# Combining two expert results per token on TensorE in a two-layer attention and expert kernel

## The chip, the cores and the metric

The kernel runs on one core of a Trainium2 chip. The metric is device microseconds of one execution, as the median of three. Before the change that is 857.17 us (runs of 855.79 to 862.05).

## The reference, cut to what matters

Two layers follow each other on 2048 tokens of 192 channels (x is 8 x 16 x 16 x 192, fp32). Each layer is an attention with a residual, then a mixture of eight experts with a residual. Of every expert layer this is what bears on the change (the first layer's; the second also divides the two gates by their sum):

```python
gates = softmax(x_flat @ Wg + bg)
topk_g, topk_i = top_k(gates, 2)             # two experts per token
combine = zeros((n, 8)).at[arange(n)[:, None], topk_i].add(topk_g)
h = gelu(einsum('nd,edf->enf', x_flat, W1) + b1)
y = einsum('enf,efd->end', h, W2) + b2
out = einsum('ne,end->nd', combine, y)       # gate-weighted sum of two results
t = t + out                                  # residual
```

After the first expert layer the sum t is layer-normalised (mean and variance over 192 channels) and goes into the second attention. After the second one it is the output.

## The kernel before

One program holds all stages; each engine has one instruction stream in program order, and semaphores order the engines among themselves. Tokens lie on partitions: 16 tiles of 128 tokens, in 4 blocks of 4 tiles (512 tokens). `x_sb` holds the residual stream, 128 x 16 x 192, in SBUF for the whole run.

In an expert layer (`moe_*`, layer l = 0 or 1) tokens are sorted by expert into 39 tiles of 128 rows, worked on in 13 trips of 3 tiles by a loop (`grouped`, whose first and last trip are written out by hand). For each trip TensorE multiplies by W1 (L1446, L1454), ScalarE applies Gelu (`hidden_units`, L1498), TensorE multiplies by W2 (L1462), VectorE adds the bias (L1342), and GpSimd scatters the rows to `yd` in DRAM (L1534), two rows per token. When the last scatter has landed, SyncE issues four loads (L1202), one per block, that bring `yd` back as `yt` (128 x 16 x 2 x 192); each signals `y_in{b}`.

The combine is then VectorE's alone (L1379 to L1394): for each block, eight `scalar_tensor_tensor` of 128 x 192 compute x = y * gate + x, first the four tiles of the first expert, then the four of the second. In layer 0 VectorE also takes the block's moments at once (`ln_moments`, L258 to L266: statistics, their aggregation, variance plus epsilon), GpSimd raises that to -1/2 (L272), and while the next block is worked on VectorE finishes scale and offset of the block before (`block_scales`, L281 to L303). ScalarE normalises the block with these into `xn` (`block_normalise`, L312), TensorE transposes it (`ln_transpose`, L323, eight transposes), ScalarE copies the transpose to SBUF (`ln_copy`, L333), and TensorE computes q, k and v (L1827). Blocks alternate between two buffers and two pairs of PSUM banks. On TensorE's stream the four `ln_transpose` stand at the head of `attn1_tensor` (L1816 and L1817), where nothing else is between them. `ln_transpose(b)` waits for `xn_ready`, and from block 2 on for the copy of block b - 2; `block_normalise` of blocks 2 and 3 waits for the transposes of two blocks earlier.

In layer 1 nothing follows the combine but the stores: SyncE waits for `combined` of a block and issues its 384 KB to the output (L1987 to L1990).

Two patterns of the second attention are like those that the change uses: twelve matmuls by the identity over 512 columns that compute nothing needed (L1892, "filler" below), and the projection, whose result VectorE adds to `x_sb` from PSUM in one instruction per block (L1806), followed by the same moments and scales.

Of the kernel before, what the change touches and what calls it, by code (L numbers as in the profile page):

```python
# [21 lines left out]
F32 = mybir.dt.float32  # L22
F32R = mybir.dt.float32r
# [3 lines left out]
ALU = mybir.AluOpType  # L27
ACT = mybir.ActivationFunctionType
# [3 lines left out]
P = 128  # L32
IMGS, SIDE, C = 8, 16, 192
PIX = SIDE * SIDE
T = IMGS * PIX
TILES = T // P
KC = 96
BLKS = 4
BT = T // BLKS
TPB = BT // P  # L40
# [12 lines left out]
HC = 3  # L53
# [12 lines left out]
R_MAX = 114  # L66
# [7 lines left out]
E, F, FT = 8, 768, 768 // P  # L74
SLOTS = 42
MT = (2 * T - E) // P + E
# [7 lines left out]
def build(nc, a, out):  # L84

    ctx = ExitStack()
    with ctx:
        def sb(name, shape, dt=F32):
            return ctx.enter_context(nc.sbuf_tensor(name, shape, dt))
# [16 lines left out]
        x_sb = sb("x_sb", [P, TILES, C])  # L106
# [3 lines left out]
        cst = sb("cst", [P, a["cst"].shape[1]])  # L110
# [17 lines left out]
        qq = sb("qq", [P, 6144], F32R)  # L128
        kk = sb("kk", [P, 6144], F32R)
        pk = sb("pk", [P, NH, PADS], F32R)  # L130
        nm = sb("nm", [HC, 2, BT], F32R)

        gw = sb("gw", [P, 2, TILES])
        gidx = sb("gidx", [P, SLOTS], I32)
# [4 lines left out]
        rt = sb("rt", [P, 2816])  # L139
        totb = sb("totb", [P, 2, P], BF16)  # L140
        hotb = sb("hotb", [P, 2 * TILES * E], BF16)
        hotb_v = hotb[:, :].rearrange("p (c e) -> p c e", e=E)
        ROUTE_STEPS = [0]
        ps = ctx.enter_context(nc.psum_tensor("ps", [P, 8, 512], F32))

        at = 0
# [10 lines left out]
        def ar(word, shape, parts=P):  # L157

            n = 1
            for s in shape:  # L160
                n *= s
            v = arena[0:parts, word:word + n]
            names = "abcd"[:len(shape)]
            if len(shape) > 1:
                v = v.rearrange(f"p ({' '.join(names)}) -> p {' '.join(names)}",
                                **{k: s for k, s in zip(names, shape)})
            return v
# [50 lines left out]
        b2s = xn[:, :, :, :].rearrange("p u t c -> p (u t) c")  # L218

        yt = ar(0, [TILES, 2, C])  # L220

        q0 = qq[:, :].rearrange("p (c h n) -> p c h n", c=CPB, h=HC)
        k0 = kk[:, :].rearrange("p (c h n) -> p c h n", c=CPB, h=HC)
# [3 lines left out]
        def s_(name):  # L227
            if name not in S:
                S[name] = sem(name)
            return S[name]  # L230
# [85 lines left out]
        def ln_transpose(pe, b):  # L316

            pe.wait_ge(s_("xn_ready"), BLKS + b + 1)
            if b >= 2:
                pe.wait_ge(s_("tp_free"), b - 1)  # L320
            for k in range(2):
                for j in range(TPB):
                    last = nc.tensor.transpose(ps[0:KC, b % 2 * 2 + k, j * P:(j + 1) * P],  # L323
                                               xn[:, b % 2, j, k * KC:(k + 1) * KC], ident)
            last.then_inc(s_("xn_free"), 1)
# [175 lines left out]
        def attn0_sync(sp):  # L501
            def load(b, cc):

                G = b * CPB + cc
                if b:
                    sp.wait_ge(s_("st_done"), (G - CPB + 1) * HC * UNITS)
                else:
                    sp.wait_ge(s_("k_rows"), cc + 1)
                sp.wait_ge(s_(f"kept_a{b}"), 8 * 16)
                if cc >= 2:  # L510
                    sp.wait_ge(s_(f"kept_b{b}"), 8 * 16)
                hs = slice(cc * HC, (cc + 1) * HC)
                for r, lo, hi in ((0, 0, 32), (R_DUP, 0, HD), (R_REL2, 32, QLO), (R_LO, QLO, QDROWS)):
                    sp.dma_start(q0[r:r + hi - lo, cc].bitcast(F32), qd[b, lo:hi, hs]).then_inc(s_(f"chunk_in{cc}"), 16)
                for r, lo in ((R_HI, 0), (R_DUP, HD), (R_LO, 0)):
                    sp.dma_start(k0[r:r + HD, cc].bitcast(F32), kd[b, lo:lo + HD, hs]).then_inc(s_(f"chunk_in{cc}"), 16)

            def minus_max(G):
                cc = G % CPB
                sp.wait_ge(s_(EMPTIED["m", G][0]), EMPTIED["m", G][1])  # L520
                sp.dma_start(q0[R_MAX:R_MAX + 1, cc].bitcast(F32), nm[0:HC, G % 2, :].bitcast(F32))\
                    .then_inc(s_(f"nm_in{cc}"), 16)

            for kind in ("t0", "t2", "r0", "r1"):
                sp.wait_ge(s_("split"), split_at(kind, 0))
                store(sp, kind, 0)
            sp.wait_ge(s_("q_rows"), CPB + 1)
            for cc in range(CPB - 1):
                load(0, cc)
            minus_max(0)  # L530
            load(0, CPB - 1)
            for b in range(BLKS):
                ahead = b + 1 < BLKS
                minus_max(b * CPB + 1)
                if ahead:
                    load(b + 1, 0)
                minus_max(b * CPB + 2)
                if ahead:
                    load(b + 1, 1)
                minus_max(b * CPB + 3)  # L540
                if ahead:
                    load(b + 1, 2)
                    minus_max(b * CPB + 4)
                    load(b + 1, 3)
            first_matrices(sp, 0, 0, E)
# [60 lines left out]
        def attn0_vector(v):  # L606
# [11 lines left out]
            def minus(G):  # L618

                v.wait_ge(s_("misc_full"), FULL["m", G])  # L620
                nc.vector.tensor_scalar(nm[0:HC, G % 2, :], ps[0:HC, BANK["m", G], :], -1.0, None, ALU.mult)\
                    .then_inc(s_("dve_emptied"), 1)

            def values(b, g):
# [530 lines left out]
        def product(r):  # L1155

            return ps[:, 2 * r, 0:C]

        def arrived(r):

            return ps[:, 6 + r // 2, r % 2 * 2 * P:(r % 2 + 1) * 2 * P].rearrange("p (k n) -> p k n", k=2)

        def grouped(eng, body):

            body(0, True, False)
            with eng.Fori(1, TRIPS - 1) as trip:
                body(trip, False, False)
            body(TRIPS - 1, False, True)
# [37 lines left out]
        def moe_vector(v, l):  # L1206
# [117 lines left out]
            if l == 1:  # L1324
# [2 lines left out]
                step(vec.reciprocal(total, total))  # L1327
                step(vec.tensor_tensor(gw[:], gw[:], total.unsqueeze(1).broadcast_to([P, 2, TILES]), ALU.mult))
            ROUTE_STEPS[0] = count[0] if l == 0 else ROUTE_STEPS[0]

            n0 = l * MT
# [44 lines left out]
                clear_columns(v)  # L1377

            for b in range(BLKS):  # L1379
                v.wait_ge(s_(f"y_in{b}"), 16 * (l + 1))  # L1380
                for k in range(2):
                    if k:
                        v.wait_ge(s_("first_added"), l * BLKS + b + 1)
                    for t in range(b * TPB, (b + 1) * TPB):
                        last = vec.scalar_tensor_tensor(x_sb[:, t], yt[:, t, k], gw[:, k, t:t + 1], x_sb[:, t],  # L1385
                                                        ALU.mult, ALU.add)
                    last.then_inc(s_("combined" if k else "first_added"), 1)
                if l == 0:
                    v.wait_ge(s_("combined"), b + 1)
                    ln_moments(v, 2, range(b, b + 1))  # L1390
                    if b:
                        block_scales(v, 2, b - 1)
# [3 lines left out]
        def moe_tensor(pe, l):  # L1396
# [68 lines left out]
            def body(trip, first, last):  # L1465
# [8 lines left out]
                for r in range(3):  # L1474
                    down(n + r, r)

            pe.wait_ge(s_("w_in"), 16 * 25 * (l + 1))
            pe.wait_ge(s_("te_ready"), l + 1)
            for r in range(3):
                gathered(n0 + r, 0, r)  # L1480
            grouped(pe, body)

        def moe_scalar(act, l):
            if l == 0:
                nx_copy(act, l, BLKS - 1)
            act.wait_ge(s_("shifted"), l + 1)
            nc.scalar.activation(rt[:, 4 * TILES * E:5 * TILES * E], rt[:, 2 * TILES * E:3 * TILES * E], ACT.Exp)\
                .then_inc(s_("exp_gates"), 1)
            if l == 0:
                clear_edges(act)  # L1490
            nc.scalar.activation(credit[0:1, 8:9], credit[0:1, 0:1], ACT.Gelu)

            def hidden_units(n, r):
                e = act.value_load(te[0:1, bass.ds(n - l * MT, 1)], min_val=0, max_val=E - 1)
                act.wait_ge(s_("up_done"), n + 1)
                act.wait_ge(s_("down_done"), n)
                for f in range(FT):
                    last = nc.scalar.activation(hidT[r][:, f, :], hidden(r, f), ACT.Gelu,  # L1498
                                                bias=b1s[l][:, bass.ds(e * FT + f, 1)])
                last.then_inc(s_("hid_ready"), 1)  # L1500

            def body(trip, first, last):
                for r in range(3):
                    hidden_units(l * MT + trip * 3 + r, r)

            act.wait_ge(s_("te_ready"), l + 1)
            grouped(act, body)
            if l == 0:
                nc.scalar.activation(credit[0:1, 8:9], credit[0:1, 0:1], ACT.Exp)
# [303 lines left out]

        def attn1_tensor(pe):
            mm = nc.tensor.matmul
            for b in range(BLKS):  # L1816
                ln_transpose(pe, b)  # L1817
            for t in range(2 * QKV_UNITS):
                image, u = unit_of(t)
                pair = t % 2  # L1820
# [365 lines left out]
```

## Time and profile before

| | |
|---|---|
| median of three runs | 857.17 us (855.79 to 862.05) |
| profiled execution | 854.11 us, of which the recorded span is 852.3 us |
| busy share of the span | TensorE 89%, weight load 77%, VectorE 48%, GpSimd 45%, ScalarE 35% |
| mean granted TensorE clock | 0.924 of full speed |
| combine of layer 0 | from 454.57 us; the last transpose behind it starts at 479.78 us |
| combine of layer 1 | from 838.15 us; its last instruction ends at 849.27 us |

### The profile page before, as it was taken

How to read it: one execution, taken by the hardware profiler on the slowest of the kernel's cores; microseconds unless marked ns; L12 is line 12 of the kernel's file. 1: busy time of each engine (PE TensorE's matmuls, PEld its weight loads, DVE VectorE, ACT ScalarE, POOL GpSimd, SP SyncE). 2: the span in 40 equal slices, each digit the busy share in tenths (PEclk: the TensorE clock that was granted, in tenths of full speed). 3: DMA queues.
4: the chain of work that ended last, by engine and by line, in shares of the span. 5: the costliest groups of instructions: out<-in, count | busy, mean ns of one | idle time of the engine just before them, and what ended most of it. 6: DMA issues, size and time to landing. Idle time of an engine off the chain costs nothing.

```text
span 852.3 us, 19475 instructions
## 1 busy us (share of the span) xinstructions
PE 760.1 (89%) x6126; PEld 658.6 (77%) x6127; DVE 413.3 (48%) x998; ACT 301.8 (35%) x858; POOL 381.6 (45%) x789
## 2 busy tenths in 40 slices
PE   8899999999977999999980689998967999999980
PEld 4687878888764999999980459683764999999980
DVE  5345554567646433334326336987346433434315
ACT  2415454545622334334240640011350424334230
POOL 8745353410314577777731030000034577777730
PEclk9759999999968999999995699999988999999995
DMA  7685664662781111111104199300882111111106
GB/s 239 184 197 124 150 156 101 162 140 55 268 331 30 41 50 50 41 58 48 54 19 148 37 266 194 60 26 25 317 331 78 39 55 51 49 55 44 50 17 222
DMA packets 61083, 97.21 MB, mean 114 GB/s; under 512 B 25712, under 2 KB 43845, under 8 KB 61033
## 3 DMA queue, kind: packets, MB, share of 16 engines
q1 hardware_dynamic: 43560, 62.28, 26.6%
q0 software_dynamic: 17472, 34.27, 13.3%
q8 instruction: 31, 0.51, 0.3%
q14 instruction: 20, 0.16, 0.1%
HBM read 66.23 MB, written 31.52 MB: 115 GB/s over the span
## 4 chain that ended last, share of the span: by engine, by line
PE 48%; issue 15%; POOL 15%; DVE 12%; DMA 5%; ACT 2%; POOLq 1%; SPq 0%; DVEq 0%
POOL credit L1516 5%; PE ps L1462 5%; PE ps L1446 5%; PE ps L756 4%; PE ps L1839 4%; POOL xnT L1524 4%; POOL yd L1534 3%; PE ps L781 3%; DVE x_sb L1385 3%; PE ps L1454 2%; PE ps L732 2%; PE ps L1857 2%; PE ps L801 2%; DVE arena L1751 2%; PE ps L825 2%
## 5 line engine op out<-in xcount | busy, mean ns | idle before, releaser
L1498 ACT ACTIVATE arena<-ps,b1s 128x128 f32<-128x128 f32 x468 | 123.6, 417 | 246.7 <-PE ps L1454 246.7
L1462 PE MATMUL ps<-arena 128*128 x936 | 158.7, 329 | 1.2 <-ACT arena L1498 1.2
L1462 PEld LDWEIGHTS ps<-arena 128*128 128x128 f32 x936 | 151.4, 190 | 3.5 <-issue 1.6
L1446 PE MATMUL ps<-xnT 128*128 128x128 f32 x936 | 113.2, 282 | 1.6 <-DVE xnT L1336 1.6
L1446 PEld LDWEIGHTS ps<-xnT 128*128 128x128 f32 x936 | 112.1, 198 | 2.4 <-DVE xnT L1336 2.4
L272 POOL TENSOR_TENSOR rstd<-veps,cst 128x4 f32<-128x4 f32 (+1 forms) x12 | 14.8, 1237 | 189.5 <-DVE veps L266 189.4
L1516 POOL TENSOR_TENSOR credit<-credit 1x1 f32<-1x1 f32 x306 | 68.0, 222 | 49.7 <-DVE xnT L1342 19.2
L1524 POOL DMA_INDIRECT xnT<-xnd,gcur x78 | 78.8, 1011 | 17.6 <-issue 12.6
L611 DVE TENSOR_REDUCE rt<-ps 98x2 f32<-98x392 f32 x96 | 53.2, 562 | 66.4 <-PE ps L781 66.3
L1348 DVE COPY xnT<-arena 128x768 f32 x78 | 43.9, 563 | 68.9 <-PE ps L1446 65.5
L1534 POOL DMA_INDIRECT yd<-rt,scur x52 | 57.7, 1109 | 29.1 <-issue 22.6
L1029 ACT ACTIVATE arena<-ps 98x392 f32<-98x392 f32 x96 | 46.8, 499 | 60.6 <-PE ps L801 60.0
L1454 PE MATMUL ps<-xnT,rt 64*128 64x128 f32 x936 | 59.3, 278 | 0.0
L1342 DVE TENSOR_TENSOR rt<-ps,xn 128x192 f32<-128x192 f32 x52 | 18.6, 358 | 80.5 <-PE ps L1462 80.5
L1454 PEld LDWEIGHTS ps<-xnT,rt 64*128 64x128 f32 x936 | 54.3, 188 | 3.1
L1839 PE MATMUL ps<-arena,cst 128*128 128x192 f32 x288 | 48.9, 334 | 3.4 <-DVE arena L1723 3.4
L1839 PEld LDWEIGHTS ps<-arena,cst 128*128 128x128 f32 x288 | 48.5, 196 | 4.2 <-DVE arena L1723 3.8
L781 PE MATMUL ps<-kk,qq 114*98 114x196 f32 x192 | 44.3, 317 | 2.0 <-DMA kk<-kd 1.7
L756 PEld LDWEIGHTS ps<-xnT,arena 128*112 128x112 f32 (+2 forms) x448 | 39.8, 179 | 6.0 <-issue 3.0
L756 PE MATMUL ps<-xnT,arena 128*112 128x32 f32 (+4 forms) x448 | 42.0, 265 | 2.0 <-POOL xnT L556 2.0
L1354 DVE COPY rt<-arena 128x384 f32 x78 | 28.2, 361 | 29.5 <-PE ps L1454 26.7
L781 PEld LDWEIGHTS ps<-kk,qq 114*98 114x98 f32 x192 | 27.7, 180 | 11.8 <-issue 9.6
(211 smaller groups left out, 1264.3 us busy)
## 6 DMA issues: line engine op xcount, KB each, us to landing
arena<-in_w SPq DMA_DIRECT2D x16, 576.0 KB, 10.9
arena<-in_w1a SPq DMA_DIRECT2D x16, 384.0 KB, 6.6
arena<-yd SPq DMA_DIRECT2D x8, 768.0 KB, 7.1
kk<-kd SPq DMA_DIRECT2D x48, 96.0 KB
qq<-qd SPq DMA_DIRECT2D x16, 264.0 KB
qq<-qd SPq DMA_DIRECT2D x16, 192.0 KB
arena<-in_w1b SPq DMA_DIRECT2D x16, 192.0 KB, 6.8
qkvd<-arena POOLq DMA_DIRECT2D x8, 384.0 KB, 8.2
```

The costliest lines, as they stand in the source:

```text
L611: m = nc.vector.tensor_reduce(mxa[0:WAH, cc, 2 * u:2 * u + 2, j], ps[0:WAH, SM + u, 0:2 * WA].rearrange("p (q n) -> p q n", q=2), AX.X, AL ...
L756: last = mm(o, relt[w][0:rows, at, 0:cols], q, start=True, stop=True)
L781: last = mm(ps[0:WAH, SM + u, c * WA:(c + 1) * WA], q[:, at:at + WAH], k[:, u * WA:(u + 1) * WA], start=True, stop=True)
L1029: e = nc.scalar.activation(pa[H % EXPS][0:WAH, u], ps[0:WAH, ST + n % 2, 0:2 * WA], ACT.Exp)
L1446: last = mm(hidden(r, f), wcura[r][:, f * P:(f + 1) * P], xgT[r][:, 0, :], start=f < 2, stop=False, skip_group_check=True)
L1454: last = mm(hidden(r, f), wcurb[r][rows, f // 2 * P:(f // 2 + 1) * P], xgT[r][rows, 1, :], start=False, stop=f >= FT - 2, skip_group_check ...
L1462: last = mm(product(r), hidT[r][:, f, :], w2s[:, e, f, :], start=f == 0, stop=f == FT - 1)
L1498: last = nc.scalar.activation(hidT[r][:, f, :], hidden(r, f), ACT.Gelu, bias=b1s[l][:, bass.ds(e * FT + f, 1)])
L1516: nc.gpsimd.tensor_tensor(credit[0:1, 12 + kind:13 + kind], credit[0:1, 0:1], credit[0:1, 0:1], ALU.add)\
L1524: nc.gpsimd.indirect_dma_start(out=xg[r], out_offset=None, in_=xnd[l], in_offset=bass.IndirectOffsetOnAxis(ap=gcur[:, r:r + 1], axis=0))\
L1534: nc.gpsimd.indirect_dma_start(out=yd[l], out_offset=bass.IndirectOffsetOnAxis(ap=scur[:, r:r + 1], axis=0), in_=ys[r], in_offset=None, bo ...
L1839: last = mm(to.rearrange("p (n x) -> p n x", n=3), ident, prod[:, 3 * col:3 * col + 3, c, :], start=c == 0, stop=c == HD - 1)
```

## The change

For every tile and each of the two experts ScalarE makes a 128 x 128 matrix that has the gates of the tile's tokens on its diagonal (identity times the gate of the partition, `diagonals`): sixteen for the first expert behind the Gelus of the first trip, sixteen for the second ahead of the Gelus of the last trip. TensorE multiplies each by the tile's expert result, and sums the two in PSUM (`combine`): eight matmuls per block, two banks, blocks alternating between banks 4, 5 and 6, 7. VectorE adds a block of 128 x 768 to the residual in one instruction. Seven fillers stand on TensorE ahead of the first combine. In layer 0 the transposes move from the attention into this order on TensorE: combine 0, combine 1, transposes 0, combine 2, transposes 1, combine 3, transposes 2, transposes 3. The tile `nm` grows from 3 to 128 partitions so that it can house diagonals; what is written and read in it stays the same.

```diff
+        GATES_MADE = [0, 0]
+        homes = [(rt, 3 * F // 2, 3 * F), (rt, 3 * F + 2 * C, 2816), ...]
+        gate_on_diagonal = [home[:, at:at + P] for home, lo, hi in homes for at in range(lo, hi - P + 1, P)]
...
+        def gated(b):
+            u = 4 + b % 2 * 2
+            return ps[:, u:u + 2, 0:2 * C]
...
             for b in range(BLKS):
-                v.wait_ge(s_(f"y_in{b}"), 16 * (l + 1))
-                for k in range(2):
-                    if k:
-                        v.wait_ge(s_("first_added"), l * BLKS + b + 1)
-                    for t in range(b * TPB, (b + 1) * TPB):
-                        last = vec.scalar_tensor_tensor(x_sb[:, t], yt[:, t, k], gw[:, k, t:t + 1], x_sb[:, t],
-                                                        ALU.mult, ALU.add)
-                    last.then_inc(s_("combined" if k else "first_added"), 1)
+                v.wait_ge(s_("gated_mm"), l * BLKS + b + 1)
+                xs = x_sb[:, b * TPB:(b + 1) * TPB, :].rearrange("p (h t) c -> p h t c", h=2)
+                vec.tensor_tensor(xs, xs, gated(b).rearrange("p h (t c) -> p h t c", t=2), ALU.add)\
+                    .then_inc(s_("combined"), 1)
                 if l == 0:
                     v.wait_ge(s_("combined"), b + 1)
                     ln_moments(v, 2, range(b, b + 1))
                     if b:
                         block_scales(v, 2, b - 1)
...
+            def combine(b):
+                pe.wait_ge(s_(f"y_in{b}"), 16 * (l + 1))
+                if b < 2:
+                    pe.wait_ge(s_("y_ready"), (l + 1) * MT)
+                    pe.wait_ge(s_("diagonals"), 2 * TILES * (l + 1))
+                else:
+                    pe.wait_ge(s_("combined"), l * BLKS + b - 1)
+                for j in range(TPB):
+                    t = b * TPB + j
+                    to = gated(b)[:, j // 2, j % 2 * C:(j % 2 + 1) * C]
+                    for k in range(2):
+                        last = mm(to, gate_on_diagonal[k * TILES + t], yt[:, t, k], start=k == 0, stop=k == 1)
+                last.then_inc(s_("gated_mm"), 1)
...
             grouped(pe, body)
+            for _ in range(7):
+                mm(ps[:, 1, :], ident, cst[:, 0:BT], start=True, stop=True)
+            for b in range(BLKS):
+                combine(b)
+                if l == 0 and b:
+                    ln_transpose(pe, b - 1)
+            if l == 0:
+                ln_transpose(pe, BLKS - 1)
...
+            def diagonals(k):
+                act.wait_ge(s_("route"), GATES_MADE[l])
+                for t in range(TILES):
+                    nc.scalar.activation(gate_on_diagonal[k * TILES + t], ident, ACT.Identity, scale=gw[:, k, t:t + 1])\
+                        .then_inc(s_("diagonals"), 1)
+
             def body(trip, first, last):
+                if last:
+                    diagonals(1)
                 for r in range(3):
                     hidden_units(l * MT + trip * 3 + r, r)
+                if first:
+                    diagonals(0)
...
         def attn1_tensor(pe):
             mm = nc.tensor.matmul
-            for b in range(BLKS):
-                ln_transpose(pe, b)
```

## Rows read from the trace of the kernel before

**Rows 1.** Page, part 4: shares of the chain that ended last.

```profile
PE 48%; issue 15%; POOL 15%; DVE 12%; DMA 5%; ACT 2%; POOLq 1%; SPq 0%; DVEq 0%
```

**Rows 2.** Chain of waits over the span: start us, us, what.

```profile
310.29 5.93 PE ps L1462 x36
...
454.57 1.42 DVE x_sb L1385 x4
...
479.78 1.94 PE ps L323 x8
481.72 8.49 PE ps L1827 x32
```

**Rows 3.** Timeline, combine of layer 0: start us, us, engine, line, instruction, count.

```profile
439.68 6.11 PE L1462 MATMUL ps<-arena 128*128 x36 [0.61 <-ACT arena L1498]
...
442.63 1.28 ACT L1509 ACT_TABLE_LOAD   x1
...
459.12 2.84 DVE L1385 SCALAR_TENSOR_TENSOR x_sb<-arena,gw,x_sb 128x192 f32<-128x192 f32 x8
...
464.36 2.84 DVE L1385 SCALAR_TENSOR_TENSOR x_sb<-arena,gw,x_sb 128x192 f32<-128x192 f32 x8
...
464.48 1.86 ACT L312 ACTIVATE xn<-x_sb,offset,rstd 128x192 f32<-128x192 f32 x4 [20.35 <-DVE offset L303]
...
466.39 1.94 PE L323 MATMUL ps<-cst,xn 128*96 128x128 f32 x8 [20.60 <-ACT xn L312]
...
471.48 1.27 ACT L333 ACTIVATE xnT<-ps 96x392 f32<-96x392 f32 x6
```

**Rows 4.** Timeline, fillers and projection of the second attention.

```profile
593.24 10.46 PE L1892 MATMUL ps<-cst 128*128 128x512 f32 x24
...
605.99 2.88 PE L1886 MATMUL ps<-wp,rt 97*128 97x192 f32 x16 [0.41 <-ACT rt L1945]
...
608.91 0.95 DVE L1806 TENSOR_TENSOR x_sb<-x_sb,ps 128x768 f32<-128x768 f32 x1 [16.24 <-PE ps L1886]
...
615.89 0.95 DVE L1806 TENSOR_TENSOR x_sb<-x_sb,ps 128x768 f32<-128x768 f32 x1
...
618.30 1.04 PE L351 MATMUL ps<-cst,xn 128*96 128x128 f32 x8
618.47 0.17 DVE L266 TENSOR_SCALAR veps<-mv 128x4 f32<-128x4 f32 x1
...
619.16 0.16 DVE L303 SCALAR_TENSOR_TENSOR offset<-mv,rstd 128x4 f32<-128x4 f32 x1
...
627.66 1.06 PE L351 MATMUL ps<-cst,arena 128*96 128x128 f32 x8
```

**Rows 5.** Windows: length, busy us per engine, PEclk (granted clock), DMA share, GB/s.

```profile
450.00:454.00 4.00, 0.00 (x0) 0.00 (x0) 0.00 (x0) 0.00 (x0) 0.00 (x0) 0.53 0.69 201
504.00:508.00 4.00, 0.58 (x4) 0.15 (x2) 3.64 (x4) 0.79 (x2) 0.66 (x2) 1.00 1.02 417
508.00:512.00 4.00, 4.00 (x15) 4.00 (x16) 4.00 (x5) 0.00 (x0) 0.00 (x0) 0.57 1.05 372
...
480.00:484.00 4.00, 4.00 (x14) 2.97 (x14) 0.00 (x0) 2.76 (x13) 0.00 (x0) 0.50 0.00 0
484.00:488.00 4.00, 4.00 (x18) 2.65 (x17) 0.00 (x0) 2.31 (x5) 0.00 (x0) 0.95 0.31 89
...
830.00:834.00 4.00, 0.00 (x0) 0.00 (x0) 0.00 (x0) 0.00 (x0) 1.61 (x5) 0.82 0.01 0
```

**Rows 6.** Timeline, last trip and combine of layer 1.

```profile
821.27 4.75 ACT L1498 ACTIVATE arena<-ps,b1s 128x128 f32<-128x128 f32 x18 [8.21 <-PE ps L1454]
...
823.08 6.11 PE L1462 MATMUL ps<-arena 128*128 x36 [0.61 <-ACT arena L1498]
...
838.15 11.12 DVE L1385 SCALAR_TENSOR_TENSOR x_sb<-arena,gw,x_sb 128x192 f32<-128x192 f32 x32 [8.46 <-DMA arena<-yd]
```

**Rows 7.** Instructions on tile yd, layer 0: the four loads of L1202.

```profile
DMA to landing us min/median/max: 4.5/7.0/9.3
```

More of the change, by code:

```diff
@@ L130, in build @@
         pk = sb("pk", [P, NH, PADS], F32R)
-        nm = sb("nm", [HC, 2, BT], F32R)
+        nm = sb("nm", [P, 2, BT])
+        gate_room = sb("gate_room", [P, F])
         gw = sb("gw", [P, 2, TILES])
@@ L220, in build @@
         yt = ar(0, [TILES, 2, C])
+        homes = [(rt, 3 * F // 2, 3 * F), (rt, 3 * F + 2 * C, 2816), (ar(E * F * 3 // 2 + 3 * F, [F]), 0, F),
+                 (nm[:, :, :].rearrange("p u n -> p (u n)"), 0, 2 * BT), (hotb[:, :].bitcast(F32), 0, P),
+                 (totb[:, :, :].rearrange("p h n -> p (h n)").bitcast(F32), 0, P), (gate_room, 0, F)]
+        gate_on_diagonal = [home[:, at:at + P] for home, lo, hi in homes for at in range(lo, hi - P + 1, P)]
         q0 = qq[:, :].rearrange("p (c h n) -> p c h n", c=CPB, h=HC)
@@ L520, in minus_max @@
                 sp.wait_ge(s_(EMPTIED["m", G][0]), EMPTIED["m", G][1])
-                sp.dma_start(q0[R_MAX:R_MAX + 1, cc].bitcast(F32), nm[0:HC, G % 2, :].bitcast(F32))\
+                sp.dma_start(q0[R_MAX:R_MAX + 1, cc].bitcast(F32), nm[0:HC, G % 2, :])\
                     .then_inc(s_(f"nm_in{cc}"), 16)
@@ L620, in minus @@
                 v.wait_ge(s_("misc_full"), FULL["m", G])
-                nc.vector.tensor_scalar(nm[0:HC, G % 2, :], ps[0:HC, BANK["m", G], :], -1.0, None, ALU.mult)\
+                nc.vector.tensor_scalar(nm[0:HC, G % 2, :].bitcast(F32R), ps[0:HC, BANK["m", G], :], -1.0, None, ALU.mult)\
                     .then_inc(s_("dve_emptied"), 1)
@@ L1329, in moe_vector @@
             ROUTE_STEPS[0] = count[0] if l == 0 else ROUTE_STEPS[0]
+            GATES_MADE[l] = count[0]
             n0 = l * MT
```

## The prediction

> **What bounds the kernel now.** I read the page's chain first: no engine bounds the whole span; TensorE carries 48% of it and VectorE 12% [rows 1]. So a gain is worth what it takes off the chain in its own stage. The chain in order of time [rows 2] shows both combines on it: in layer 0 it runs from VectorE's first instruction at 454.57 to the last group of transposes at 479.78 and on into q, k and v; whatever moves 479.78 moves all that follows, because the second attention has no other input. In layer 1 the 32 instructions of VectorE take 838.15 to 849.27 [rows 6], and only stores follow. The timeline then gives the prices, and the windows the granted clock.
>
> One block now costs VectorE 2.84 us for eight instructions [rows 3], and with its moments and the scales of the block before the cadence in layer 0 is 5.24 us (459.12 to 464.36 [rows 3]). TensorE waits in this stage: 20.60 us before the first transposes [rows 3].
>
> **Parts that cost nothing on the path.** The diagonals are 16 activations of 128 x 128 in each of two places per layer. Nearest rows: 18 Gelus of that size from PSUM take 4.75 us, 0.264 each [rows 6]; four 128 x 192 with a scale per partition from SBUF take 1.86, 0.465 each [rows 3]. So 16 take 4.2 to 7.4 us. ScalarE idles 8.21 us between two trips [rows 6], and both places lie in such a gap, so I take 0. That cover fails if the switch between Gelu and Identity loads tables: two loads of 1.28 us [rows 3] make it 6.8 to 10.0, that is up to 1.8 late, in four places up to 7.2. Identity runs at L312 after the exp table was loaded at L1509 [rows 3] and no other load stands between, so the one switch that rows show needs none; I stay at 0. The Trainium skill (ScalarE: Activation LUTs, Table sets: the hidden batching unit) says that identity is in every table set; by that the 7.2 is excluded, and no row shows it for Gelu's set. The seven fillers are 14 records of 10.46 / 24 = 0.436 us [rows 4], 6.1 us; behind the last L1462, at 445.79 and 829.19 [rows 3, 6], they end at 451.9 and 835.3, before the first block of `yt` is there (454.57 and 838.15), so they delay nothing. The wider `nm` changes no instruction's size. The loads of blocks 1 to 3 land up to 9.3 us after issue against 4.5 for the first [rows 7], about 2 us or less apart, and don't hold a combine of 2.64 us.
>
> **Layer 1.** A block is 8 matmuls, 16 records. L1462 has the same stationary and 192 columns: 36 records in 5.93 us, 0.165 each [rows 2], so 2.64 per block, and 2.88 where nothing follows, as for the 16 of the projection [rows 4]. Four blocks end 3 x 2.64 + 2.88 = 10.80 after 838.15, at 848.95; the add of 128 x 768 starts 0.04 later and takes 0.95 [rows 4]. It ends at 849.94, against 849.27 now: **0.7 us later**. TensorE needs 2.64 for what VectorE did in 2.78, and the add comes on top.
>
> **Layer 0.** VectorE's work per block falls to the projection's: from the start of an add to the offset of the block before is 619.32 - 615.89 = 3.43 us [rows 4]. But the moved transposes sit in TensorE's stream between the combines. Transposes 0 wait for ScalarE's normalise of block 0, which waits for block 0's scales, which VectorE makes after the add and the moments of block 1. Behind them on TensorE waits combine 2, whose inputs are long there; behind combine 2 waits VectorE's add 2, and behind that the scales that transposes 1 need. What ran side by side becomes one circle: add, moments and scales 3.43, normalise 1.86 [rows 3], transposes, combine, and again, with some 0.04 at each hand-over.
>
> The clock sets the rest. TensorE idles 0.04 + 3.43 + 0.04 + 1.86 + 0.05 = 5.4 us per circle. Rows 5 show it at half speed 4.4 us after the last matmul in layer 0 (the mean 0.53 of 450 to 454 puts the fall at 450.24) and 3.4 us after in layer 1 (0.82: fall at 832.56). So transposes run at half, 1.94 [rows 3], not 1.04 [rows 4]. The clock rose at 484.4 (0.95 in 484 to 488), 4.6 us after the transposes of 479.78 had started [rows 2, 5]. By that, combine runs 2.66 us at half, 8 records of 0.33, then 8 of 0.165: 4.0 us. Bounds: 2.64 if the clock doesn't fall, 5.28 if it doesn't rise again.
>
> In order: combines 0 and 1 end at 454.57 + 2.64 + 2.88 = 460.09. Moments of block 0 hold VectorE until 460.20 (457.45 + 2.75, as 615.89 to 618.64 [rows 4]); add 1, moments 1 and scales 0 end at 463.63, normalise 0 at 465.53, transposes 0 run 465.58 to 467.52, combine 2 to 471.66 with 0.16 of drain. Second circle: scales 1 at 475.13, normalise 1 at 477.03, transposes 1 to 479.02, combine 3 to 483.16. Then scales 2 at 486.63, normalise 2 at 488.53; ScalarE copies transposes 1 next in its stream, 1.27 [rows 3], and normalises block 3, until 491.66. Transposes 3 start at 491.71, against 479.78 now: **11.9 us later**. Everything behind is as before. At full clock throughout, the same steps give 487.23, +7.5; with no rise in a combine 494.3, +14.5.
>
> **Sum.** 11.9 + 0.7 = 12.6 us. On the profiled execution, 854.11 (span 852.3 and 1.8 around it), that is 866.7. The median of the runs lies 3.06 above that execution, so I forecast 857.17 + 12.6 = 869.8.
>
> **Rivals.** First, not slower: the waiting transposes don't hold the combines, because TensorE takes ready work past them. Then the projection is the pattern: from its first add at 608.91 to its last transposes at 627.66 are 18.75 us [rows 4]; from add 0 at 457.45 that gives 476.2, 3.6 us earlier than now; with 0.7 in layer 1 the time is 854.3. It decides if transposes 0 start after combine 2. For it: the work is ready. Against it: in these rows every matmul stands in program order. The Trainium skill (TensorE: Matmul & The Clock Gate, What happens when you issue a matmul) says matmuls stay in program order and only weight loads are pulled ahead. By that this rival falls away and the circle stands; no row here has ready work behind a wait to show it.
>
> Second, the clock stays up, since what TensorE does in a circle is enough: +7.5 + 0.7 = 8.2, 865.4. For it: a fall took 4.4 us in layer 0, not far from the 5.4 idle here. Against: 3.4 us idle in 504 to 508 sufficed for a fall at the head of 508 to 512 (0.57) [rows 5].
>
> Third, the fillers don't hold the clock. They leave 454.57 - 451.9 = 2.7 and 838.15 - 835.3 = 2.9 us idle. After the 3.4 us of 504 to 508 the clock was at half for 0.43 / 0.5 x 4 = 3.4 us [rows 5]. At that price each layer loses half of 3.4, together 3.4: 873.2. The gaps are shorter than any after which rows show a fall, so it is less likely.
>
> Fourth, tables are loaded around the diagonals, at up to 7.2 and, with 0.41 per diagonal (0.465 less the time of 64 columns), nearer 4: about 874.
>
> **Chances.** The circle with half clock in its transposes 0.66; clock stays up 0.13; fillers fail 0.07; tables 0.04; not slower 0.10. A measurement of this kernel can tell about 1%, 8.6 us, from no change: the bound is 865.7. The clock case lies on it, so I count half of it on either side: slower 0.66 + 0.07 + 0.04 + 0.06 = 0.83. The first rival is within 1% mostly: 0.08 + 0.07 = 0.15, and 0.02 faster. The range reaches down to the clock case on the profiled execution's own base, 854.1 + 8.2 = 862, and up to the third and fourth rivals, 875; the not slower case, 0.10, is left out.
>
> **What will show it.** Right: TensorE's order in layer 0 has transposes 0 ahead of combine 2 with some 5.4 us idle before each group of transposes, named to ScalarE's normalise; VectorE waits for TensorE before adds 2 and 3, where it hardly waits now; blocks come every 11.4 us; the last transposes start near 491.7; granted clock 0.5 in them, 1.0 in combines 0 and 1. VectorE's busy time falls by 8 x 2.84 - 8 x 0.95 = 15 us and the time rises all the same. Layer 1 ends within a microsecond of where it did after its loads land. Wrong: transposes at 1.04 us (the second rival), combines of over 2.9 us in layer 1 (the third), table loads next to the diagonals or a later L1498 in first or last trips (the fourth). I would be wrong outright if transposes 0 came after combine 2, or if scales 0 didn't need block 1's add.

## The result and the profile after

The changed kernel takes 869.40 us in the median of 20 executions (856.29 to 874.08), the kernel before 857.63 in as many (853.47 to 862.05): a ratio of medians of 1.0137, 11.8 us slower. A ratio that is given with a 95% interval, here 1.0083 (1.0055 to 1.0111), compares only the executions within 1.5% of each kernel's fastest, so it can differ from that of the medians beside it, and in the row "the same again" below it leaves out the longer 7 of 13. By either, the change costs time. The forecast was 869.8, in a range of 862 to 875. The profiled execution is one of 871.73 us with a span of 869.9.

The page of the changed kernel, first its parts 1 (busy us, share, count) and 4 (shares of the chain). VectorE's busy time fell from 413.3 to 400.1, by 13.2 us of the 15 forecast, TensorE's rose from 760.1 to 798.8, and VectorE's share of the chain stayed at 12% [rows 1].

```profile
PE 798.8 (92%) x6282; PEld 686.7 (79%) x6283; DVE 400.1 (46%) x942; ACT 320.8 (37%) x922; POOL 381.0 (44%) x789
...
PE 43%; POOL 16%; issue 15%; DVE 12%; DMA 6%; SPq 3%; ACT 2%; POOLq 1%; DVEq 0%
```

The timeline of layer 0, the lines that answer to [rows 3] (line numbers moved: L1496 is the combine, L1394 its add, L1505 the fillers, L318 the normalise, L329 the transposes):

```profile
445.93 6.17 PE L1505 MATMUL ps<-cst 128*128 128x512 f32 x14
...
454.89 1.01 PE L1496 MATMUL ps<-arena,rt 128*128 128x192 f32 x2 [2.79 <-DMA arena<-yd]
...
460.42 0.95 DVE L1394 TENSOR_TENSOR x_sb<-x_sb,ps 128x768 f32<-128x768 f32 x1 [12.61 <-PE ps L1496]
...
463.41 0.95 DVE L1394 TENSOR_TENSOR x_sb<-x_sb,ps 128x768 f32<-128x768 f32 x1 [0.25 <-PE ps L1496]
...
466.88 1.86 ACT L318 ACTIVATE xn<-x_sb,offset,rstd 128x192 f32<-128x192 f32 x4 [22.45 <-DVE offset L309]
...
468.80 1.94 PE L329 MATMUL ps<-cst,xn 128*96 128x128 f32 x8 [5.42 <-ACT xn L318]
...
475.38 0.95 DVE L1394 TENSOR_TENSOR x_sb<-x_sb,ps 128x768 f32<-128x768 f32 x1 [8.54 <-PE ps L1496]
...
480.76 1.94 PE L329 MATMUL ps<-cst,xn 128*96 128x128 f32 x8 [5.41 <-ACT xn L318]
...
486.50 0.95 DVE L1394 TENSOR_TENSOR x_sb<-x_sb,ps 128x768 f32<-128x768 f32 x1 [7.69 <-PE ps L1496]
...
491.88 1.94 PE L329 MATMUL ps<-cst,xn 128*96 128x128 f32 x8 [5.42 <-ACT xn L318]
...
494.81 1.94 PE L329 MATMUL ps<-cst,xn 128*96 128x128 f32 x8 [0.99 <-ACT xn L318]
```

This is the circle. TensorE waits 5.4 us for ScalarE ahead of each of the first three groups of transposes, and VectorE waits 8.54 and 7.69 us for TensorE ahead of adds 2 and 3, though those blocks had long been loaded. Before, the first three groups stood 5.2 us apart, the first at 466.39 [rows 3] and the next two here:

```profile
471.62 1.94 PE L323 MATMUL ps<-cst,xn 128*96 128x128 f32 x8 [3.29 <-ACT xn L312]
...
476.86 1.94 PE L323 MATMUL ps<-cst,xn 128*96 128x128 f32 x8 [3.29 <-ACT xn L312]
```

Now they start at 468.80, 480.76 and 491.88. The last starts at 494.81 instead of 479.78 [rows 2].

The chain of waits gives what the combines themselves took, and the windows (length, busy us of five engines, then granted clock) say why they took so much:

```profile
454.89 8.49 PE ps L1496 x32
...
470.73 4.63 PE ps L1496 x16
...
482.70 3.78 PE ps L1496 x16
```

```profile
452.00:456.00 4.00, 1.21 (x4) 1.11 (x4) 0.00 (x0) 0.00 (x0) 0.00 (x0) 0.78 0.98 356
456.00:460.00 4.00, 4.00 (x14) 4.00 (x14) 0.00 (x0) 0.00 (x0) 0.00 (x0) 0.50 1.06 372
460.00:464.00 4.00, 3.37 (x18) 3.07 (x16) 3.23 (x11) 0.00 (x0) 0.74 (x1) 0.87 0.14 49
464.00:468.00 4.00, 0.00 (x0) 0.00 (x0) 2.64 (x14) 1.12 (x3) 1.32 (x2) 0.98 0.00 0
468.00:472.00 4.00, 3.21 (x13) 3.14 (x14) 0.00 (x0) 0.74 (x2) 0.00 (x0) 0.50 0.02 4
```

The clock fell at 454.24 (0.78 of the first window), 2.1 us after the fillers had ended, and rose at 461.04 (0.87 of the third). So combines 0 and 1 took 8.49 us instead of 5.52. It fell again behind combine 1, before transposes 0 began.

In layer 1 the same fillers left the same gap, 2.76 us, and the clock held (granted 1.00 from 835 to 870 us):

```profile
855.23 0.59 PE L1496 MATMUL ps<-arena,rt 128*128 128x192 f32 x2 [2.76 <-DMA arena<-yd]
...
858.13 0.95 DVE L1394 TENSOR_TENSOR x_sb<-x_sb,ps 128x768 f32<-128x768 f32 x1 [11.17 <-PE ps L1496]
...
865.93 0.95 DVE L1394 TENSOR_TENSOR x_sb<-x_sb,ps 128x768 f32<-128x768 f32 x1 [1.65 <-PE ps L1496]
```

The last add ends 866.88 - 855.23 = 11.65 us after the first block was there, 0.5 later than VectorE alone had it (11.12 [rows 6]).

### The profile page after: what moved, and what is told of

It is laid out like the page before. It is cut to its first block, busy times and chain, and to the rows that moved or that the text cites. A ratio compares the mean times of both kernels' runs of the same rounds, so it can differ in the third digit from the quotient of the medians.

```text
span 869.9 us, 19803 instructions
## 1 busy us (share of the span) xinstructions
PE 798.8 (92%) x6282; PEld 686.7 (79%) x6283; DVE 400.1 (46%) x942; ACT 320.8 (37%) x922; POOL 381.0 (44%) x789
## 4 chain that ended last, share of the span: by engine, by line
PE 43%; POOL 16%; issue 15%; DVE 12%; DMA 6%; SPq 3%; ACT 2%; POOLq 1%; DVEq 0%
POOL credit L1556 5%; PE ps L1454 5%; PE ps L1470 5%; POOL xnT L1564 4%; PE ps L762 4%; PE ps L1496 3%; POOL yd L1574 3%; DVE arena L1791 3%; PE ps L1462 2%; PE ps L787 2%; SPq L1690 2%; PE ps L1430 2%; PE ps L807 2%; PE ps L831 2%; PE ps L738 2%
## 5 line engine op out<-in xcount | busy, mean ns | idle before, releaser
L1564 POOL DMA_INDIRECT xnT<-xnd,gcur x78 | 78.9, 1011 | 17.6 <-issue 12.8
L762 PEld LDWEIGHTS ps<-xnT,arena 128*112 128x112 f32 (+2 forms) x448 | 34.9, 166 | 7.3 <-POOL xnT L562 3.7
L762 PE MATMUL ps<-xnT,arena 128*112 128x32 f32 (+4 forms) x448 | 37.5, 255 | 2.6 <-POOL xnT L562 2.6
L1895 PE MATMUL ps<-arena,cst 128*128 128x512 f32 (+3 forms) x84 | 34.4, 561 | 3.5 <-DVE arena L1821 3.3
```

What stands on the lines that cost most here:

```text
L762: last = mm(o, relt[w][0:rows, at, 0:cols], q, start=True, stop=True)
L1564: nc.gpsimd.indirect_dma_start(out=xg[r], out_offset=None, in_=xnd[l], in_offset=bass.IndirectOffsetOnAxis(ap=gcur[:, r:r + 1], axis=0))\
```

## The experiments

The time of a whole execution mixes this stage with others whose clock differs. So each trace was cut at the same places, and the table has the lengths: **P** from the start of the span to the first expert matmul of layer 0, **A** from the end of the last down product of layer 0 to the start of the last transposes (the stage that changed), **B** from there to the fillers ahead of the projection, **C** from those to the first expert matmul of layer 1, **E** from the last down product of layer 1 to the end. **R** is all that stands behind P. The 13 trips of layer 0 between P and A took 170.6 to 171.3 us in all traces, those of layer 1 between C and E 171.3 to 171.9. Medians are over 11 to 13 executions (6 without fillers, 20 in the first two rows); "before" is the median of the kernel before on the same chip.

| kernel | median us | before | ratio, 95% interval | P | A | B | C | E | R |
|---|---|---|---|---|---|---|---|---|---|
| before | 857.63 | | | 274.79 | 33.99 | 113.46 | 64.44 | 23.11 | 577.51 |
| changed | 869.40 | 857.63 | 1.0083, 1.0055 to 1.0111 | 274.85 | 48.71 | 113.90 | 65.90 | 23.46 | 595.07 |
| all transposes last | 862.45 | 856.99 | 1.0076, 1.0039 to 1.0112 | 274.59 | 29.39 | 116.60 | 72.04 | 25.26 | 585.48 |
| the same again | 861.50 | 856.75 | 0.9946, 0.9904 to 0.9987 | 285.96 | 29.39 | 116.91 | 72.00 | 23.55 | 584.47 |
| one block ahead | 853.20 | 856.99 | 0.9979, 0.9946 to 1.0011 | 284.61 | 34.77 | 113.94 | 65.99 | 23.52 | 581.41 |
| clock held | 866.32 | 856.99 | 1.0099, 1.0056 to 1.0141 | 279.19 | 41.05 | 112.44 | 75.19 | 23.54 | 594.70 |
| no fillers | 872.10 | 856.99 | 1.0142, 1.0080 to 1.0204 | 273.63 | 48.71 | 113.05 | 64.58 | 25.68 | 594.64 |
| layer 1 only | 857.19 | 856.75 | 0.9987, 0.9954 to 1.0021 | 279.46 | 34.04 | 113.48 | 64.30 | 25.34 | 579.46 |
| before, router held | 853.51 | 856.75 | 0.9939, 0.9902 to 0.9977 | 273.43 | 34.06 | 113.62 | 64.29 | 23.00 | 577.52 |
| last, split in layer 1, router held | 854.10 | 856.75 | 0.9980, 0.9944 to 1.0016 | 277.04 | 29.41 | 114.29 | 64.68 | 21.40 | 571.71 |
| last, router held | 855.57 | 856.91 | 0.9964, 0.9923 to 1.0005 | 280.45 | 29.48 | 116.91 | 65.65 | 25.27 | 579.55 |
| last, split, held throughout | 848.36 | 856.91 | 0.9924, 0.9884 to 0.9963 | 271.67 | 29.51 | 113.70 | 65.66 | 20.31 | 571.72 |

Nothing of any edit runs in P: every trace has the same number of instructions of each engine there. Yet P differs by up to 14.3 us between traces, and the mean granted clock with it. The windows of its shortest ("last, split, held throughout") and its longest ("the same again"), with the engines in the order TensorE, weight load, VectorE, ScalarE, GpSimd:

```profile
0.00:271.67 271.67, 248.75 (x2387) 196.75 (x2389) 150.61 (x388) 122.46 (x261) 112.82 (x160) 0.92 0.61 167
0.00:285.96 285.96, 260.71 (x2388) 207.64 (x2389) 150.69 (x388) 122.17 (x261) 112.89 (x160) 0.87 0.59 158
```

TensorE is busy 12.0 us longer in the second, the other three engines as long. So of two traces R is compared, not the whole time: 577.51 us before, 595.07 in the changed kernel, 17.6 more.

### All transposes last

```diff
             for b in range(BLKS):
                 combine(b)
-                if l == 0 and b:
-                    ln_transpose(pe, b - 1)
             if l == 0:
-                ln_transpose(pe, BLKS - 1)
+                for b in range(BLKS):
+                    ln_transpose(pe, b)
```

> The changed kernel with the four groups of transposes of layer 0 behind all four combines on TensorE, so that no combine stands behind a wait for ScalarE. The circle's theory: the add, moments and scales of a block (3.43 us) set the pace as in the projection, the last transposes start near 476 to 479, and the time is 854 to 858 us, some 12 to 15 below the changed kernel's 869.4. Rival, the combine on TensorE costs the time in itself (diagonals on ScalarE, matmuls at half clock): it stays at 865 or above.

The timeline of its transposes:

```profile
464.96 1.08 PE L329 MATMUL ps<-cst,xn 128*96 128x128 f32 x8 [0.27 <-ACT xn L318]
...
468.29 1.08 PE L329 MATMUL ps<-cst,xn 128*96 128x128 f32 x8 [2.25 <-ACT xn L318]
...
471.62 1.94 PE L329 MATMUL ps<-cst,xn 128*96 128x128 f32 x8 [2.26 <-ACT xn L318]
...
474.55 1.94 PE L329 MATMUL ps<-cst,xn 128*96 128x128 f32 x8 [0.98 <-ACT xn L318]
```

The first three come 3.3 us apart, VectorE's pace, the last start is at 474.55 where 476 to 479 was expected, and A is 29.39 us: 19.3 less than changed and 4.6 less than before. For the stage the circle's theory is right and the rival false, since the combine on TensorE, the diagonals and the matmuls are all still there. For the whole it missed: 862.45, not 854 to 858. B is 3.1 us longer than before and C 7.6, in code that no edit touches, and E 2.2, because the clock fell in the combine of layer 1, as it did not in the changed kernel.

### One block ahead

```diff
-                if l == 0 and b:
-                    ln_transpose(pe, b - 1)
+                if l == 0 and b > 1:
+                    ln_transpose(pe, b - 2)
             if l == 0:
-                ln_transpose(pe, BLKS - 1)
+                for b in range(BLKS - 2, BLKS):
+                    ln_transpose(pe, b)
```

> The changed kernel with the order combine 0, 1, 2, transposes 0, combine 3, transposes 1, 2, 3. The circle's theory: one combine still stands behind one wait, so one turn of the circle is left in part: transposes 0 can start near 465.5 while combine 3 could have started at 462.7, and add 3 comes 3 to 5 us later than with all transposes last; 858 to 862 us. Rival: moving transposes between combines is not what costs, 869.

```profile
478.62 1.08 PE L329 MATMUL ps<-cst,xn 128*96 128x128 f32 x8 [2.82 <-ACT xn L318]
...
482.14 1.04 PE L329 MATMUL ps<-cst,xn 128*96 128x128 f32 x8
482.34 0.95 DVE L1394 TENSOR_TENSOR x_sb<-x_sb,ps 128x768 f32<-128x768 f32 x1 [2.33 <-PE ps L1496]
...
490.64 1.94 PE L329 MATMUL ps<-cst,xn 128*96 128x128 f32 x8 [1.12 <-ACT xn L318]
```

This execution also began its combines at half clock (combines 0 and 1 took 8.45 us), so it stands directly beside the changed one: from the first combine, at 464.77, to the last transposes it took 25.9 us, against 494.81 - 454.89 = 39.9. One block of distance removes 14.0 us. What is left of the circle is VectorE's 2.33 us ahead of add 3, less than the 3 to 5 expected, and the median, 853.20, is below the expected 858. B and C are as in the changed kernel (113.94 and 65.99 against 113.90 and 65.90). R is 581.41, 13.7 less than changed and 3.9 more than before, of which the half clock in combines 0 and 1 makes 3.0. So a gain against the kernel before is not shown: the interval holds 1.

### Clock held

```diff
-            for _ in range(7):
+            for _ in range(9):
                 mm(ps[:, 1, :], ident, cst[:, 0:BT], start=True, stop=True)
             for b in range(BLKS):
                 combine(b)
                 if l == 0 and b:
+                    for _ in range(5):
+                        mm(ps[:, (0, 1, 2, 4)[b], :], ident, cst[:, 0:BT], start=True, stop=True)
                     ln_transpose(pe, b - 1)
```

> The changed kernel in its own order, with five fillers (ten records of 0.43 us) ahead of transposes 0, 1 and 2 and nine instead of seven ahead of the combines, so that TensorE is busy while it would wait. If the clock makes up the part of the circle that the prediction gave to it: transposes at 1.04 and combines at 2.64 us, the last transposes 7.5 us behind the kernel before, 865 to 866 us, and less spread between runs. If the clock plays no part: 869, as the changed kernel. If fillers push transposes back because they run at half speed: above 870.

```profile
464.38 4.45 PE L1510 MATMUL ps<-cst 128*128 128x512 f32 x10
...
470.02 1.08 PE L329 MATMUL ps<-cst,xn 128*96 128x128 f32 x8 [1.18 <-ACT xn L318]
...
479.11 1.08 PE L329 MATMUL ps<-cst,xn 128*96 128x128 f32 x8 [1.12 <-ACT xn L318]
...
488.21 1.08 PE L329 MATMUL ps<-cst,xn 128*96 128x128 f32 x8 [1.12 <-ACT xn L318]
```

With TensorE busy through its waits every group of transposes takes 1.08 us and the first three are 9.1 us apart. Behind the fillers TensorE still waits 1.1 to 1.2 us for ScalarE, so they delayed nothing. A is 41.05, 7.1 us more than before, where the prediction's second rival gave 7.5. So of the 14.7 us that the change added to A, 7.06 are the circle at full speed and 7.66 the clock; 3.0 of these are combines 0 and 1, which leaves 4.7 for the circle's own half clock, 4.4 in the prediction (11.9 less 7.5). That the median, 866.32, is the expected 866 is in part luck: the trace lost in C what it gained in A. Its R is 594.70, as in the changed kernel, since C is 75.19. The clock fell in the router of layer 1:

```profile
628.00:632.00 4.00, 2.07 (x16) 1.77 (x16) 3.76 (x20) 2.37 (x7) 1.01 (x1) 0.97 1.05 409
632.00:636.00 4.00, 4.00 (x19) 3.77 (x18) 1.50 (x11) 3.48 (x9) 3.61 (x5) 0.50 1.02 411
```

### No fillers

```diff
-            for _ in range(7):
-                mm(ps[:, 1, :], ident, cst[:, 0:BT], start=True, stop=True)
```

> The changed kernel without the seven fillers ahead of the combines. If they hold the clock for the first combines in most executions: combines 0 and 1 of layer 0 and the first of layer 1 run at half speed in all of them, 2 to 5 us more than the changed kernel, 871 to 875. If the gap behind the fillers lets the clock fall anyway, or the loss in layer 0 is hidden: 869.

A is 48.71, as in the profiled execution of the changed kernel, which had the fillers and lost the clock all the same. E is 25.68 against 23.46: the combine of layer 1 at half clock for a while costs 2.2 us. The median of 872.10 is of 6 executions from 864 to 882 and can't be told from 869.40, so what the fillers gain in the changed kernel isn't shown.

### Layer 1 only

```diff
+                if l == 0:
+                    v.wait_ge(s_(f"y_in{b}"), 16 * (l + 1))
...
+            if l == 1:
+                for _ in range(7):
+                    mm(ps[:, 1, :], ident, cst[:, 0:BT], start=True, stop=True)
+                for b in range(BLKS):
+                    combine(b)
+            else:
+                for b in range(BLKS):
+                    ln_transpose(pe, b)
...
-                if last:
+                if last and l == 1:
                     diagonals(1)
```

> The change in layer 1 alone: layer 0 combines on VectorE and transposes as in the kernel before. The circle's theory puts the whole loss into layer 0: this is within 1 us of the kernel before, 857 to 858, and its stretch from the last down product of layer 0 to the last transposes is the 34.0 us of before. Rival, the combine on TensorE costs the time in itself: half of the loss stays, 863.

857.19 against 856.75, ratio 0.9987 (0.9954 to 1.0021), and A is 34.04. The loss is layer 0's. Layer 1 neither gains nor loses what can be told, though E is 25.34 in its profile, 2.2 more than before: the clock fell 1.1 us behind the start of the combine.

### Where the gain of "all transposes last" went

The same kernel was run again:

> The same kernel as the one with all transposes last, timed once more, because its stretch in layer 0 became 4.6 us shorter than before while its median was 5 us longer. If the loss behind that stretch is the clock's, which falls in the layer-1 router in some executions and not in others, a second set of executions spreads as widely and its median need not be the same: 852 to 862. If it belongs to this order of instructions, the median comes out at 862 again.

The median came out at 861.50, and a second trace has the same lengths, A 29.39, B 116.91, C 72.00. The two spans differ by 10.3 us, P by 11.4 and R by 1.0 the other way. The expectation isn't decided by this, because 861.50 lies in both of its ranges, and 6 of the 13 executions took 848.63 to 856.06. In C the windows of this second trace show the layer-1 router:

```profile
628.00:632.00 4.00, 2.07 (x18) 1.78 (x17) 3.74 (x20) 2.70 (x6) 1.01 (x1) 0.99 1.05 410
632.00:636.00 4.00, 4.00 (x20) 3.80 (x18) 1.16 (x7) 3.49 (x9) 4.00 (x5) 0.50 1.01 407
```

and those of the kernel before, 12.0 us behind its own projection, the same place:

```profile
618.00:622.00 4.00, 2.07 (x18) 1.78 (x18) 3.73 (x21) 2.64 (x6) 1.01 (x1) 1.00 1.03 406
622.00:626.00 4.00, 3.86 (x34) 3.67 (x31) 1.20 (x8) 3.48 (x9) 3.94 (x5) 1.00 1.03 414
```

TensorE's work is the same up to there, 2.07 us in 4, but in the one the clock falls at the end of it and in the other it doesn't, and the next 4 us hold 20 records instead of 34. To test this, two fillers went into that gap, as the only other edit:

```diff
                 nx_transpose(pe, l, 0)
+                for _ in range(2):
+                    mm(ps[:, 5, :], ident, cst[:, 0:BT], start=True, stop=True)
                 for b in range(BLKS):
```

> All transposes last, and as the only other edit the two fillers of 512 columns in the layer-1 router. Two profiles of the order without them had 72.0 us from the projection's fillers to the first expert matmul of layer 1, against 64.4 before, with the clock at half in the router. If the clock there is what gave the gain of layer 0 back: that stretch is 64.4 to 65 again, layer 0 keeps its 29.4, and the median falls by some 7 from 862 to 854 to 856. If the loss belongs elsewhere: 860 to 862.

```profile
626.00:630.00 4.00, 3.86 (x35) 3.72 (x34) 1.65 (x13) 3.48 (x9) 3.47 (x5) 1.00 1.02 411
630.00:634.00 4.00, 4.00 (x36) 3.90 (x34) 0.00 (x0) 3.47 (x8) 3.55 (x5) 1.00 1.03 401
```

The clock holds, C is 65.65 instead of 72.0, A is 29.48, and the median is 855.57, 6 to 7 below the two sets without the fillers. For the traced executions that is shown: the gain of layer 0 was given back by the clock of the layer-1 router, some 145 us further on. In how many executions isn't known, since 6 of the 13 of the second set lie within 0.5 us of the median with the fillers, or below it. R is 579.55, still 2.0 more than before; this lies in B, again 116.91, and in E. In B q, k and v took 10.53 us in the chain instead of 8.49, and the channel sums 34.37 instead of 33.15.

The same two fillers in the kernel before:

> The kernel before with two fillers of 512 columns in the gap of TensorE in the layer-1 router (behind the first transposes there). If executions differ because the clock falls in that gap in some of them: the slow tail of the kernel before (860 to 867) goes, median 854 to 856, the stretch from the projection's fillers to the first expert matmul stays at 64.4 us. If the clock there is the same in all executions: 857, with the same spread.

This settles nothing: 853.51 is as expected, but C is 64.29, as without them, R is 577.52 against 577.51, and executions still differ by 16 us. Nothing behind P accounts for the 3 us of the median.

### Two versions built on this

The first has all transposes last, both fillers of the router, and each block of layer 1 split, two tiles on each engine:

```diff
+                    for k in range(2):
+                        for t in range(b * TPB, b * TPB + 2):
+                            last = vec.scalar_tensor_tensor(x_sb[:, t], yt[:, t, k], gw[:, k, t:t + 1], x_sb[:, t], ...)
...
+                    xs = x_sb[:, b * TPB + 2:(b + 1) * TPB, :].rearrange("p t c -> p (t c)")
+                    vec.tensor_tensor(xs, xs, gated(b)[:, 1], ALU.add).then_inc(s_("combined"), 1)
...
-                for j in range(TPB):
+                for j in range(2 * l, TPB):
```

> Three edits on the changed kernel: all transposes of layer 0 last, each block of layer 1 split (two tiles on VectorE as before, two on TensorE with one add of 128 x 384), and the two fillers in the layer-1 router. Layer 0 gains 4 us against before; in layer 1 the loads of yt, 2.1 us apart, become the pace: the last add ends some 8.3 us after the first load instead of 11.1, 2.8 less. Together 850 us, below both kernels. If the loads land later than that because the stores run beside them, layer 1 gains 1 us or nothing: 853. If the loss behind the stretch in layer 0 belongs to that order, 857 to 860.

```profile
836.20 1.53 DVE L1403 SCALAR_TENSOR_TENSOR x_sb<-arena,gw,x_sb 128x192 f32<-128x192 f32 x4 [8.35 <-DMA arena<-yd]
...
845.18 0.55 DVE L1409 TENSOR_TENSOR x_sb<-x_sb,ps 128x384 f32<-128x384 f32 x1
```

A 29.41 and C 64.68 came as expected. The combine of layer 1 took 845.73 - 836.20 = 9.5 us, not 8.3, because the clock fell 1.0 us behind its start and stayed at half for 3.4, and E is 21.40, 1.7 less than before instead of 2.8. R is 571.71, 5.8 less than before, but the median, 854.10, is no difference from before that can be told. The second adds two fillers ahead of the combines, and two behind each of the first three groups of transposes:

```diff
-            for _ in range(7):
+            for _ in range(9):
...
                 for b in range(BLKS):
                     ln_transpose(pe, b)
+                    for _ in range(2 if b < BLKS - 1 else 0):
+                        mm(ps[:, 2 + 2 * b, :], ident, cst[:, 0:BT], start=True, stop=True)
```

> All transposes last, layer 1 split between VectorE and TensorE, two fillers in the layer-1 router, nine fillers ahead of the combines, and two fillers behind each of the first three groups of transposes of layer 0, so that the q, k, v matmuls start at full speed. If the clock is what is left to gain there: the q, k, v group takes 7 us instead of the 8.5 of before and 10.4 with all transposes last, the stretch from the last transposes to the projection's fillers 111 to 112 instead of 113.5, and the median is 848 to 850. If ScalarE's copies and not the clock bound q, k and v, it stays at 114 and the median at 853 to 854.

```profile
451.77 2.88 PE ps L1512 x16
...
474.81 6.48 PE ps L1882 x28
...
499.53 34.30 PE ps L1894 x192
```

```profile
473.23 1.03 PE L1882 MATMUL ps<-xnT,wqkv 96*96 96x256 f32 x4
...
831.83 1.53 DVE L1403 SCALAR_TENSOR_TENSOR x_sb<-arena,gw,x_sb 128x192 f32<-128x192 f32 x4 [8.24 <-DMA arena<-yd]
...
839.81 0.56 DVE L1409 TENSOR_TENSOR x_sb<-x_sb,ps 128x384 f32<-128x384 f32 x1
```

848.36, 8.6 us below the kernel before (ratio 0.9924, 0.9884 to 0.9963) and 21 below the changed one: it beats both. R accounts for 5.8 of the 8.6. It is 571.72, the same as in the first version: these two traces differ by P alone, and what in the edits makes their medians 5.7 us apart isn't shown. The combine of layer 1 takes 840.37 - 831.83 = 8.5 us instead of 11.1, paced by the loads, 2.1 apart. Combine 0 takes 2.88 us, as expected. For q, k and v the chain has 6.48, but of 28 records; all 32 took from 473.23 to 481.29, 8.1 us, against 8.7 before (481.51 to 490.21), not 7. And B is 113.70, not 111 to 112, so that part of the expectation fell: the load behind them took 8.14 us instead of 7.59, and the channel sums (L1894) 34.30 instead of 33.15, with the clock at half for 6.8 us at their start instead of 3.4.

## Why the prediction was right, point by point

**The circle.** Its mechanism is as predicted: transposes 0 ahead of combine 2, adds 2 and 3 waiting for TensorE. The idle time ahead of transposes was put at 5.4 us and is 5.41 to 5.42. Transposes were put at 1.94 us and are. Combines 2 and 3 were put at 4.0 (4.14 with the drain) and took 4.63 and 3.78; the distance between groups, put at 11.5, is 11.96 and 11.12. Moving the transposes to the end, or one block ahead, takes the loss in A away, so this is shown.

**Its size.** The last transposes were put 11.9 us later and are 15.0 later in the profiled execution. The term that was off is combines 0 and 1: put at 5.52, they took 8.49. The third rival, that fillers don't hold the clock, came true in layer 0 of this execution and not in layer 1, with the same gap. Its price was low too: 1.7 us per layer, from 3.4 us at half speed; the clock was at half for 6.8 us here, which costs 3.0. Without this the forecast of 491.71 would have been met within a few tenths. So the sign "granted clock 1.0 in combines 0 and 1" failed, and the chance of this rival, 0.07, was too low: over all traces with the seven fillers, which left gaps of 2.8 to 3.0 us, the clock fell in the gap or up to 1.4 us behind it in 6 of 13; with nine fillers and gaps of 1.0 to 1.3 us in none of 4.

**Layer 1.** Put at 0.7 later, measured 0.5. Where the clock falls at its start, E is 25.3 to 25.7 instead of 23.5, about 2 us, near the 1.7 of the third rival.

**Parts that cost nothing.** The sixteen diagonals took 4.8 to 4.9 us in each of the four places, inside the 4.2 to 7.4, and 3.55 us of the gap of 8.2 are left here. ScalarE's timeline in the last trip of layer 0:

```profile
429.84 2.45 ACT L1535 ACTIVATE nm<-cst,gw 128x128 f32<-128x128 f32 x8
...
432.75 1.87 ACT L1535 ACTIVATE gate_room<-cst,gw 128x128 f32<-128x128 f32 x6
438.17 2.17 ACT L1528 ACTIVATE arena<-ps,b1s 128x128 f32<-128x128 f32 x8 [3.55 <-PE ps L1462]
```

No table is loaded beside them (the whole trace has four loads, as before), so the fourth rival is out, and the sentence of the Trainium skill on identity (ScalarE: Activation LUTs, Table sets: the hidden batching unit) agrees with this trace. The 13 trips of layer 0 took 171.25 us against 171.00.

**The first rival.** TensorE didn't take combine 2 past transposes 0, which waited 5.42 us ahead of it with combine 2's inputs there: its block had landed at 459.08 and add 0, which frees its banks, ended at 461.37. That is the row that was missing, and it agrees with what the Trainium skill (TensorE: Matmul & The Clock Gate, What happens when you issue a matmul) says of matmuls, that they stay in program order. The stage that this rival priced, 3.6 us shorter than before, is what the order with all transposes last gave (4.6).

**The sum.** For the median 12.6 us were forecast and 11.8 measured. For the profiled execution it is 871.73 - 854.11 = 17.6: 14.7 in A, 0.4 in B, 1.5 in C, 0.3 in E, and 0.6 in the trips of both layers with the 0.1 ahead of them. P is the same in these two traces (274.79 and 274.85). So the near match of the medians is partly luck: the traced pair lost 5 us more than the forecast, 3.0 of them in combines 0 and 1 and 1.5 in C, and the changed kernel's executions spread over 18 us, of which one was traced. The prediction left the clock in the other stages as it was, and it isn't.

## What to carry to other kernels

When work is moved to an in-order engine, look at what stands between its pieces in that engine's stream: a piece that waits for the result of its neighbour makes a circle, and one block of distance between the two was worth 14 us here. A stage that becomes shorter need not make the kernel shorter: cut the traces at the same places and compare stage by stage, since the clock of a sparse stage some 145 us further on gave all of it back until two fillers held it. Leave out what runs ahead of every edit: here that stretch alone differed by 14 us between traces, more than the change was worth in the medians.

## What the runs showed of the hardware that wasn't expected

The same gap of 2.8 us behind the same fillers lost the clock in layer 0 (fall at 454.24, 6.8 us at half) and kept it in layer 1 of the same execution. The two traces of "all transposes last" agree and disagree: in the layer-1 router the clock fell at the same place in both (C 72.04 and 72.00), in the combine of layer 1 in one alone (E 25.26 and 23.55). So two traces suggest, and don't show, that a fall can belong to an order of instructions. "Clock held" lost it in the router too (C 75.19), one block ahead didn't (65.99); why stays open. That executions of one kernel differ by some 16 us fits what the traces place in P: 271.67 us at a mean granted clock of 0.92 and 285.96 at 0.87, with the same instructions. What sets the clock there stays open.
